# An AdaLN attention and mixture kernel: where the first batch forms its modulations, and when GpSimd builds its one-hot tables

## Chip, cores and metric

The kernel runs on one NeuronCore of a Trainium2 chip. The metric is device time in microseconds of the whole launch; lower is better. PE is TensorE, PEld its weight loads, DVE is VectorE, ACT is ScalarE, POOL is GpSimd, SP is SyncE, which here only issues DMAs.

## What is computed

The input x has 8 batches of 512 tokens with 128 channels, in fp32. Two blocks follow each other. The first is attention (8 heads of 16 channels, a top-102 emphasis of the scores, a mean over queries, a small convolution and a softmax) and a mixture of 8 experts; the second is a Mamba layer and a second mixture of 8 experts with a capacity. Both are wrapped by adaptive layer norms, whose shifts, scales and gates come from a small matrix product, once for all batches:

```python
def _layernorm(x, axis=-1, eps=1e-05):
    m = jnp.mean(x, axis=axis, keepdims=True)
    v = jnp.var(x, axis=axis, keepdims=True)
    return (x - m) / jnp.sqrt(v + eps)
...
    mod = (_silu(L0_c) @ L0_wmod).reshape(L0_c.shape[0], 6, 1, -1)
    sa, ca, ga, sb, cb, gb = (mod[:, 0], mod[:, 1], mod[:, 2], mod[:, 3], mod[:, 4], mod[:, 5])
    ga = (2 * (ga >= 0) - 1) * jnp.maximum(jnp.abs(ga), 0.25)
    gb = (2 * (gb >= 0) - 1) * jnp.maximum(jnp.abs(gb), 0.25)
    h = _layernorm(x, axis=-1) * (1 + ca) + sa
    x = x + ga * _L0_attn_ref(h, ...)
    h = _layernorm(x, axis=-1) * (1 + cb) + sb
    x = x + gb * _L0_ffn_ref(h, ...)
    mod = (_silu(L1_c) @ L1_wmod).reshape(L1_c.shape[0], 6, 1, -1)
    ...
    h = _layernorm(x, axis=-1) * (1 + ca) + sa
    x = x + ga * _L1_attn_ref(h, ...)
    h = _layernorm(x, axis=-1) * (1 + cb) + sb
    x = x + gb * _L1_ffn_ref(h, ...)
    return x
```

## The kernel before

The work of a batch is two chains. **The attention chain** prepares a batch (layer norm, the K and Q projections, a bounce of Q and K through DRAM and back into the tile qk), fills 32 score tiles of 128x512 (lines 698 on PE and 732 on ACT), and searches in five rounds for each row's threshold (line 765 on DVE, line 747 on ACT, with a few small DVE instructions such as line 772 between the rounds). The last small instruction of the search, line 781, writes g_bad. PE then runs one tiny matmul on g_bad, line 816, DVE reads its result (lines 868 to 882), and the choice phase begins: for each of the 32 tiles PE forms the scores again and masks them (lines 698 and 828), DVE takes the eight best and marks them (lines 900, 907 and 891), POOL turns the marks into weights (line 934) and PE gathers with them (line 844). A softmax phase follows, and line 1118 on DVE adds the result to x: with it a batch's attention is over.

**The rest chain** does everything else for a batch. Experts of the first mixture are pairs of fp32 matmuls, line 1307 (up) and line 1297 (down), 32 of each per batch, with a spread of the gate (line 1149) for each expert and a product on POOL between (line 1367). The Mamba part runs 32 scans (line 1566) and products (lines 1578 and 1606) with identity matmuls that sum them on PE (line 1523). Line 1138 adds the result to x, then come a layer norm, a router with many small DVE instructions (lines 1672 to 1711), and the experts of the second mixture (lines 1749, 1751, 1763 and 1828). Line 1844 adds their result and line 1864 sends the batch out.

Each engine executes its queue in order. The order in which the two chains are written into each queue is decided when the kernel is built, by `weave`: it steps through generators that yield either a signal they need or a number, an assumed duration, and keeps an assumed clock for each engine. It takes the generator that could start first; among those within 0.05 of each other it takes the one whose chain is behind. A chain's progress is the sum of the yielded numbers over its total (532.0 for the rest chain, 467.5 for the attention chain), less its lead (0.0 and 1.25). So an additional yielded number moves both the engine's assumed clock and the balance between the chains, for the whole program.

Ahead of the woven part each engine runs a setup. SP issues all loads. ACT takes the silu of the conditioning vector and the exponential of A_log. PE forms the modulation products (two groups, signal `modp`) and one product with the bias. DVE clears tables, then `dve_setup` forms the modulations from PE's two groups: 9 small instructions each, at lines 372 to 381, then lines 384 and 385. The last is the fifth rise of the signal `ready`. `started` makes every engine wait for `built`, `cleared`, `ready` and `loaded`. POOL's first work after it is `pool_one_hots` (lines 337 to 342), which builds the tables onehot and stacker; its generator then yields 20.0. The first batch's layer norm is `dve_norm` on DVE (statistics at lines 448 and 452, variance at 455), a power of -0.5 on POOL (`pool_norm`, line 467) and the normalisation on DVE at line 460.

## Time and profile before

| what | us |
|---|---|
| median of 3 runs | 3219.97 |
| lowest and highest of them | 3219.43 and 3223.93 |
| time of the profiled execution | 3232.89 |
| span of the profiled execution | 3231.7 |

The first two lines are times of ordinary executions. The profile shows another execution, of which the span is what lies between its first and its last instruction; 1.19 us of its time lie outside. The rows below come from that execution, so they are compared with its own time.

### The profile page before, as it was taken

Reading aid. Unit: us, or ns where it says so; the run is one execution under the profiler, and the core shown is the slowest. Engines: PE = TensorE matmul, PEld = TensorE weight load, DVE = VectorE, ACT = ScalarE, POOL = GpSimd, SP = SyncE. Lnnn points to the kernel's source line nnn. Section 1 sums busy time; section 2 is a strip of 40 time slices with the busy share of each in tenths; the row PEclk is TensorE's granted clock in tenths of the full one; section 3 lists DMA queues with packets and bytes.
Section 4 is the critical chain, followed back from the end, with each engine's and each line's share of the span. In section 5 each row is a group of like instructions: output and inputs, shape, how many; then the busy total and the mean of one; then the engine's idle time right before and its main releaser. Section 6 shows DMA issues by size and latency. Waiting matters only on the chain.

```text
span 3231.7 us, 34184 instructions
## 1 busy us (share of the span) xinstructions
PE 2248.2 (70%) x8658; PEld 1163.9 (36%) x8767; DVE 2569.1 (79%) x6529; ACT 1554.1 (48%) x3348; POOL 1224.5 (38%) x1118
## 2 busy tenths in 40 slices
PE   4068396877868687777768777777867778668644
PEld 2015132544234432444235522445325532345213
DVE  5974887889888898879888897979889897954482
ACT  3406633675256733676145843567236752534322
POOL 1020053623544154523544154532535144533461
PEclk8579597888978888878978788788979879779757
DMA  4011012232132312322133211323121421313222
GB/s 96 0 25 31 0 40 78 75 76 75 44 91 69 96 49 61 88 69 86 47 84 76 84 54 54 93 58 93 56 75 63 102 58 47 91 31 113 73 69 91
DMA packets 137464, 215.15 MB, mean 67 GB/s; under 512 B 17872, under 2 KB 57440, under 8 KB 134112
## 3 DMA queue, kind: packets, MB, share of 16 engines
q1 hardware_dynamic: 133088, 203.88, 23.0%
q0 software_dynamic: 4096, 8.40, 0.9%
q14 instruction: 209, 1.71, 0.2%
q8 instruction: 71, 1.16, 0.2%
HBM read 190.06 MB, written 22.15 MB: 66 GB/s over the span
## 4 chain that ended last, share of the span: by engine, by line
DVE 38%; PE 23%; issue 21%; POOL 6%; ACT 5%; DMA 2%; another core or an unknown queue 2%; DVEq 2%; SPq 1%; POOLq 0%; ACTq 0%
DVE wmask L765 13%; PE ps_att L1018 3%; DVE best L900 3%; PE ps_rest L1297 3%; PE ps_rest L1307 3%; DVE hg L1578 2%; DVE hfc L1566 2%; PE ps_att L1029 2%; POOL gat L1606 2%; DVEq L902 2%; PE ps_rest L1523 1%; PE ps_rest L1393 1%; DMA cols<-slots 1%; ACT wmask L747 1%
## 5 line engine op out<-in xcount | busy, mean ns | idle before, releaser
L765 DVE TENSOR_SCALAR_CACHE_REDUCE wmask<-z,tc 128x512 bf16<-128x512 f16 x640 | 438.8, 740 | 25.0 <-ACT z L732 22.8
L1367 POOL TENSOR_TENSOR gat<-sil,cbs 128x512 f32<-128x512 f32 x256 | 324.8, 1270 | 181.8 <-PE ps_rest L1297 114.2
L1332 ACT ACTIVATE sil<-ps_rest,w_b1T 128x512 f32<-128x512 f32 x256 | 175.7, 687 | 443.5 <-PE ps_rest L1307 424.0
L1018 PE MATMUL ps_att<-z,Vp 128*32 128x128 f32 x2048 | 290.8, 291 | 42.6 <-DVE z L1090 27.6
L934 POOL TENSOR_SCALAR wmask<-wmask 128x512 bf16<-128x512 bf16 x256 | 162.4, 634 | 381.3 <-DVE wmask L891 375.2
L1619 POOL TENSOR_TENSOR rest_c<-rest_c,hg 128x512 f32<-128x512 f32 x128 | 162.5, 1269 | 362.2 <-DVE hg L1578 362.2
L1307 PE MATMUL ps_rest<-rest_hT,WF 128*128 128x512 f32 x512 | 286.3, 646 | 7.4 <-ACT sil L1332 7.3
L1297 PE MATMUL ps_rest<-gat,WP 128*128 128x512 f32 x512 | 273.2, 617 | 6.5 <-POOL gat L1367 5.6
L1018 PEld LDWEIGHTS ps_att<-z,Vp 128*32 128x32 f32 x2048 | 213.9, 116 | 141.4 <-issue 120.6
L1523 PE MATMUL ps_rest<-hg,ident 128*128 128x512 f32 x256 | 184.1, 809 | 115.0 <-DVE hg L1578 114.8
L1068 DVE CUSTOM_DVE_ANT_0 z<-ps_att,wmask 128x512 f32<-128x512 f32 x256 | 174.9, 683 | 105.5 <-PE ps_att L1006 80.1
L1546 ACT ACTIVATE ps_rest<-cols,Aneg 128x512 f32<-128x512 f32 x256 | 175.5, 688 | 171.7 <-DVE hfc L1566 151.8
L698 PE MATMUL ps_att<-qk 128*128 128x512 bf16 x476 | 211.6, 460 | 47.0 <-DMA qk<-bounce 24.9
L1578 DVE TENSOR_TENSOR hg<-hfc,ccs 128x512 f32<-128x512 f32 x256 | 224.7, 880 | 2.6 <-POOL rest_c L1619 2.6
L467 POOL TENSOR_TENSOR rest_rstd<-rest_vpe,halfs 128x4 f32<-128x4 f32 x40 | 40.7, 1019 | 480.8 <-DVE rest_vpe L455 480.8
L900 DVE MAX8 best<-ps_att 128x8 f32<-128x512 f32 x256 | 177.3, 692 | 56.2 <-PE ps_att L828 46.8
L891 DVE SCALAR_TENSOR_TENSOR wmask<-ps_att,g_v,wmask 128x512 bf16<-128x512 f32 x256 | 192.1, 750 | 24.3 <-DVE pick L907 17.2
L1606 POOL TENSOR_TENSOR gat<-cols,cbs 128x512 f32<-128x512 f32 x128 | 179.0, 1399 | 71.9 <-DVE cols L1484 68.3
L1029 PE MATMUL ps_att<-ident,z 128*128 128x128 f32 x1024 | 178.4, 301 | 38.6 <-ACT z L1056 37.8
L1047 ACT ACTIVATE z<-z,nmx 128x512 f32<-128x512 f32 x256 | 184.9, 722 | 8.4
L1749 PE MATMUL ps_rest<-cols,WF 128*128 128x153 f32 x512 | 133.9, 346 | 71.4 <-DVE gat L1828 31.6
L1606 POOL TENSOR_TENSOR rest_c<-cols,cbs 128x512 f32<-128x512 f32 x128 | 174.8, 1366 | 0.0
(347 smaller groups left out, 5025.7 us busy)
## 6 DMA issues: line engine op xcount, KB each, us to landing
cbs<-spreads SPq DMA_DIRECT2D x128, 256.0 KB, 3.7
ccs<-spreads SPq DMA_DIRECT2D x128, 256.0 KB, 3.4
WF<-in_w SPq DMA_DIRECT2D x64, 256.0 KB, 2.6
WP<-in_w SPq DMA_DIRECT2D x64, 256.0 KB, 2.7
WF<-in_wfc SPq DMA_DIRECT2D x64, 256.0 KB, 2.6
WG<-in_wgate SPq DMA_DIRECT2D x64, 256.0 KB, 2.9
WP<-in_wproj SPq DMA_DIRECT2D x64, 256.0 KB, 3.3
qk<-bounce SPq DMA_DIRECT2D x32, 384.0 KB, 5.7
```

The lines of the kernel that those rows point to most:

```text
L698: return pe.matmul(bank[:], qs[:, h, j * P:(j + 1) * P], ks[:, h, :], start=True, stop=stop)
L765: od.up(dve.tensor_scalar(wmask[:, i, :], z_at[i], tc[:, 0, i:i + 1], None, ALU.is_ge, ALU.add, accum_out=tc[:, 1, i:i + 1]))
L891: masked.up(dve.scalar_tensor_tensor(wmask[:, i - 1, :], xbank[(i - 1) % 3][:], g_["v"][:, i - 1:i], wmask[:, i - 1, :], ALU.is_ge, ALU.add))
L900: od.up(dve.max(best[u][:, 0:8], xbank[i % 3][:]))
L1018: mm = pe.matmul(obank[o:o + 32, a * P:(a + 1) * P], Vp[:, kc, h, :], pT[u][:, kc, :], start=kc == 0, stop=kc == NT - 1)
L1029: mm = pe.transpose(in_tiles(tbank)[:, kc, :], prob[n % 2][:, kc * P:(kc + 1) * P], ident[:])
L1297: down0.up(pe.matmul(bk[3][:], W2[e % 2][:, c, :], gat[(n - 3) % 2], start=False, stop=False))
L1307: up0.up(pe.matmul(bk[n % 2][:], W1[e % 2][:, c * P:(c + 1) * P], rest.hT[:], start=True, stop=True))
L1367: weighed0.up(pool.tensor_tensor(gat[m % 2], sil[m % 2], cbs[e % 2][:], ALU.mult))
L1523: summedY.up(pe.matmul(bk[2][:], ident[:], hc[0], start=False, stop=False))
L1578: seen.up(dve.tensor_tensor(hc[k], hs[k], ccs[s % 3][:], ALU.mult))
L1606: inputs.up(pool.tensor_tensor(dBx[2 * k + s % 2], dtx[:, k, :], cbs[s % 4][:], ALU.mult))
```

## The change

The statistics of the first batch's layer norm are written ahead of the modulations on DVE, and the modulations come between the variance and the wait for POOL's power. POOL builds its one-hot tables in its setup, ahead of `started`. DVE, POOL and SP no longer wait for `ready`. Two yielded numbers change as well: the 20.0 behind the one-hot tables goes, and a 5.0 behind the modulations comes.

```diff
@@ dve_setup
         ready.up(dve.tensor_scalar(wts["bq"][:], wts["bq"][:], SCALE, None, ALU.mult))
+
+    def dve_modulations():
+
         for l in range(2):
             dve.wait_ge(*modp.at(0, l))
@@ started
         eng.wait_ge(*cleared.all(0))
-        eng.wait_ge(*ready.all(0))
+        if eng in (pe, act):
+            eng.wait_ge(*ready.all(0))
         eng.wait_ge(*loaded.all(0))
@@ dve_norm
-    def dve_norm(w, b, k, src):
+    def dve_norm(w, b, k, src, meanwhile=None):
@@
         w.var.up(dve.tensor_scalar(w.vpe[:], w.mv[:, :, 1], LN_EPS, None, ALU.add))
         yield 0.21
+        if meanwhile:
+            meanwhile()
+            yield 5.0
         yield w.rooted.at(b, k)
@@ dve_rows
-        yield from dve_norm(att, b, 0, xr[b % 3])
+        yield from dve_norm(att, b, 0, xr[b % 3], None if b else dve_modulations)
@@ pool_rest
     def pool_rest():
-        pool_one_hots()
-        yield 20.0
         for b in every:
@@
-    sp_setup(); pool_setup(); act_setup(); pe_setup(); dve_setup()
+    sp_setup(); pool_setup(); pool_one_hots(); act_setup(); pe_setup(); dve_setup()
```

The built program has the same instructions on every engine in another order. Line numbers of the changed kernel are higher by 3 from line 372 on, by 4 at lines 448 to 455 and by 7 from line 460 on. Three places show how the order changed.

The first is DVE's queue at the end of its setup. Before, the last modulations stand ahead of the statistics of the first batch's norm:

```order
L380 TENSOR_TENSOR modT<-stA,sgn 128x8
L381 TENSOR_TENSOR modT<-stA,sgn 128x8
L384 TENSOR_TENSOR bo<-ps_att,w_bo 128x1
L385 TENSOR_SCALAR gbo<-modT,bo 128x8
L448 BN_STATS att_stats<-xr 128x6 x4
L452 BN_AGGR att_mv<-att_stats 128x2 x4
L455 TENSOR_SCALAR att_vpe<-att_mv 128x4
L460 TENSOR_SCALAR att_nrm<-xr,att_mv,att_rstd 128x128 x4
```

Now, with 14 rows of modulations left out at the mark:

```order
L369 TENSOR_SCALAR w_bq<-w_bq 128x1
L452 BN_STATS att_stats<-xr 128x6 x4
L456 BN_AGGR att_mv<-att_stats 128x2 x4
L459 TENSOR_SCALAR att_vpe<-att_mv 128x4
L375 COPY modT<-ps_att 128x48
...
L384 TENSOR_TENSOR modT<-stA,sgn 128x8
L387 TENSOR_TENSOR bo<-ps_att,w_bo 128x1
L388 TENSOR_SCALAR gbo<-modT,bo 128x8
L467 TENSOR_SCALAR att_nrm<-xr,att_mv,att_rstd 128x128 x4
```

The three rows of the statistics moved ahead of all the modulations; what follows the normalisation is the same.

The second place is PE's queue around the matmul on g_bad, where the search of batch 4 (the fifth batch, counted from 0) ends. WP and WF are the expert weights, ps_att3 takes the result. Before:

```order
L1307 MATMUL ps_rest1<-rest_hT,WF_1 128x512
L1149 MATMUL ps_rest2<-cpart,onehot 128x512
L1297 MATMUL ps_rest3<-gat,WP_0 128x512
L1307 MATMUL ps_rest0<-rest_hT,WF_1 128x512
L1297 MATMUL ps_rest3<-gat,WP_1 128x512
L1307 MATMUL ps_rest1<-rest_hT,WF_1 128x512
L816 MATMUL ps_att3<-g_bad,ones_col 1x32
L1297 MATMUL ps_rest3<-gat,WP_1 128x512
L1307 MATMUL ps_rest0<-rest_hT,WF_0 128x512
L698 MATMUL ps_att0<-qk 128x512
```

Now:

```order
L1304 MATMUL ps_rest3<-gat,WP_0 128x512
L1314 MATMUL ps_rest1<-rest_hT,WF_0 128x512
L1304 MATMUL ps_rest3<-gat,WP_0 128x512
L1314 MATMUL ps_rest0<-rest_hT,WF_1 128x512
L1304 MATMUL ps_rest3<-gat,WP_0 128x512
L823 MATMUL ps_att3<-g_bad,ones_col 1x32
L1314 MATMUL ps_rest1<-rest_hT,WF_1 128x512
L1156 MATMUL ps_rest2<-cpart,onehot 128x512
L1304 MATMUL ps_rest3<-gat,WP_0 128x512
L705 MATMUL ps_att0<-qk 128x512
```

The matmul on g_bad moved back in PE's queue, past more expert matmuls. Of the batch's 32 up and 32 down matmuls 16 and 13 stood ahead of it; now it is 21 and 19, and one more spread. In batches 2 to 7 together 61 more expert matmuls and 8 more spreads stand ahead of it, in batch 1 it is 13 and 1.

The third place is DVE's queue around line 1118 (now 1125), the end of the last batch's attention. Before:

```order
L1588 SCALAR_TENSOR_TENSOR rest_c<-cols,w_m_D,rest_c 128x512
L1590 TENSOR_TENSOR hg<-rest_c,cols 128x512
L1118 TENSOR_TENSOR xr<-xr,ps_att 128x512
L1138 TENSOR_TENSOR xr<-xr,ps_rest 128x512
L448 BN_STATS rest_stats<-xr 128x6 x4
L452 BN_AGGR rest_mv<-rest_stats 128x2 x4
```

Now:

```order
L1168 TENSOR_REDUCE sv_m<-sm_t 128x4
L1169 TENSOR_TENSOR oh<-sm_t,sv_m 128x32
L1125 TENSOR_TENSOR xr<-xr,ps_att 128x512
L1687 TENSOR_TENSOR sm_oh<-oh 128x32
L1689 TENSOR_TENSOR sv_s<-sv_v 128x4
```

Behind the last line 1118 DVE had 337 instructions left, all of the rest chain; it now has 311. The 26 between them, from line 1138 to the second group of router instructions (line 1162), moved ahead of it.

## Rows read from the trace of the kernel before

**Rows 1.** The page's busy times of the whole span, with shares and instructions
```profile
PE 2248.2 (70%) x8658; PEld 1163.9 (36%) x8767; DVE 2569.1 (79%) x6529; ACT 1554.1 (48%) x3348; POOL 1224.5 (38%) x1118
```

**Rows 2.** Windows: one batch of the overlapped stretch, and the end
```profile
core 0: us, PE busy (x) PEld busy (x) DVE busy (x) ACT busy (x) POOL busy (x), PEclk, DMA share, GB/s
1408.00:1779.00 371.00, 278.27 (x1076) 144.78 (x1089) 317.43 (x797) 192.74 (x418) 150.89 (x136) 0.83 0.26 71
2873.00:3231.00 358.00, 200.66 (x708) 113.03 (x709) 165.32 (x337) 111.33 (x205) 145.51 (x119) 0.73 0.27 81
```

**Rows 3.** Timeline of the start: start, duration, engine, line, [idle before <-releaser]
```profile
8.35 0.47 SPq L295 DMA_DIRECT2D xr<-in_x  x1
...
15.43 0.21 DVE L372 COPY modT<-ps_att 128x48 f32<-128x48 f32 x1 [1.07 <-PE ps_att L355]
...
18.07 0.21 DVE L372 COPY modT<-ps_att 128x48 f32<-128x48 f32 x1 [0.94 <-PE ps_att L355]
...
19.91 0.23 DVE L385 TENSOR_SCALAR gbo<-modT,bo 128x8 f32<-128x8 f32 x1
...
20.32 0.87 DVE L448 BATCH_NORM_STATS2 att_stats<-xr 128x6 f32<-128x128 f32 x4 [0.19 <-DVE gbo L385]
20.35 0.95 POOL L337 MEMSET onehot<- 96x1024 bf16 x1 [14.78 <-DVE gbo L385]
...
21.65 0.17 DVE L455 TENSOR_SCALAR att_vpe<-att_mv 128x4 f32<-128x4 f32 x1
...
26.53 1.05 POOL L467 TENSOR_TENSOR att_rstd<-att_vpe,halfs 128x4 f32<-128x4 f32 x1
27.62 1.11 DVE L460 TENSOR_SCALAR att_nrm<-xr,att_mv,att_rstd 128x128 f32<-128x128 f32 x4 [5.80 <-POOL att_rstd L467]
```

**Rows 4.** Source view of line 295, which loads the first batch's x
```profile
DMA to landing us min/median/max: 4.8/4.8/4.8
```

**Rows 5.** Windows: the stretch ahead of the bounce transfers
```profile
30.00:35.00 5.00, 4.79 (x10) 2.73 (x11) 1.82 (x5) 1.53 (x3) 0.00 (x0) 1.00 0.00 0
```

**Rows 6.** Waits of PE from 672 to 2873 us: total, times, longest
```profile
PE ps_rest L1523 <- DVE hg L1578: 54.6, 24, 8.9
...
PE ps_att L816 <- DVE g_bad L781: 42.3, 6, 8.0
```

**Rows 7.** Waits of DVE in the same stretch
```profile
DVE best L900 <- PE ps_att L828: 34.6, 40, 2.3
```

**Rows 8.** Timeline of PE in the batch from 1408 us
```profile
1511.12 0.38 PE L1149 MATMUL ps_rest<-cpart,onehot 96*128 96x512 bf16 x1
...
1513.09 1.02 PE L1307 MATMUL ps_rest<-rest_hT,WF 128*128 128x512 f32 x2
...
1514.80 1.02 PE L1307 MATMUL ps_rest<-rest_hT,WF 128*128 128x512 f32 x2
...
1542.29 0.26 PE L816 MATMUL ps_att<-g_bad,ones_col 128*1 128x32 f32 x2 [6.92 <-DVE g_bad L781]
...
1544.35 1.91 PE L1307 MATMUL ps_rest<-rest_hT,WF 128*128 128x512 f32 x2
```

**Rows 9.** Windows: batch 1's choice; then six microseconds of batch 4's
```profile
440.00:500.00 60.00, 59.56 (x156) 21.33 (x157) 42.80 (x95) 17.46 (x27) 39.76 (x44) 0.98 0.19 54
1542.00:1548.00 6.00, 5.49 (x10) 2.17 (x12) 4.23 (x14) 0.69 (x1) 1.40 (x1) 0.50 0.07 23
```

**Rows 10.** Timeline of DVE: two issues of line 772 in batch 4
```profile
1470.58 0.16 DVE L772 TENSOR_SCALAR tc<-tc 128x14 f32<-128x14 f32 x1
...
1513.62 1.09 DVE L772 TENSOR_SCALAR tc<-tc 128x14 f32<-128x14 f32 x1
```

**Rows 11.** Timeline of POOL beside the second of them
```profile
1510.81 3.88 POOL L1367 TENSOR_TENSOR gat<-sil,cbs 128x512 f32<-128x512 f32 x3 [5.70 <-ACT sil L1332]
```

**Rows 12.** Timeline of DVE where the last batch's attention ends
```profile
2872.06 0.69 DVE L1118 TENSOR_TENSOR xr<-xr,ps_att 128x512 f32<-128x512 f32 x1 [2.24 <-PE ps_att L1105]
...
2883.38 0.19 DVE L1162 TENSOR_TENSOR oh<-sm_t,sv_m 128x32 bf16<-128x32 f32 x1
```

## The prediction

> **What bounds the kernel now.** I read the busy shares first. DVE is busy 79% of the span, PE 70%, ACT and POOL less than half [rows 1]. The windows say where that holds: a batch in the overlapped stretch takes 371 us and DVE is busy 317 of them, while the last 358 us, in which the rest chain runs alone, keep DVE busy for only 165 [rows 2]. So the kernel has three kinds of time: a start that is a pure chain of waits, seven batches in which DVE is nearly full, and an end that is a chain again. A microsecond taken from the start or the end counts whole. In the middle only DVE's waits can be won or lost.
>
> The start is next. In its timeline the normalisation of the first batch (line 460) waits 5.80 us for POOL's power, the power stands behind the one-hot tables, and these wait 14.78 us for line 385, the last rise of `ready` [rows 3]. That is the chain which the diff speaks of. The waits of the middle are third, since the order listings show that the change reaches there: PE waits 42.3 us in six pieces at line 816 for the end of the search, and DVE waits 34.6 us in 40 pieces for the masked scores of line 828 [rows 6, 7].
>
> **The start.** DVE is through with line 369 at 15.43 - 1.07 = 14.36 us. The first batch's x was issued at 8.35 and took 4.8 to land, so it is there at 13.15 [rows 3, 4]. The statistics can start at 14.36. They took from 20.32 to 21.65 + 0.17 = 21.82, that is 1.50 us, and will end at 15.86. The first group of modulations lasts from 15.43 to 18.07 - 0.94 = 17.13, 1.70 us; it now runs from 15.86 to 17.56. The second group waits for PE's products, which let it go at 18.07 [rows 3], and PE is not touched. So the slack of 0.51 us swallows the displaced group, and line 385 ends at 19.91 + 0.23 = 20.14 as before. POOL's power takes 1.05 us [rows 3] and runs at about 16 to 17 beside the modulations. The normalisation starts at about 20.2 in place of 27.62: 7.4 us earlier.
>
> The one-hot tables cost nothing where they now stand. They took POOL from 20.35 to 26.53, 6.2 us, and POOL was idle for 14.78 us before them, since 5.6 us [rows 3]; they end at about 12, ahead of the power at 15.9. Without that cover they would cost their 6.2 us, which is what they cost before. The waits that DVE, POOL and SP lose are of no further price. PE and ACT keep theirs, and both are released at 20.14 ahead of their first work.
>
> One thing can take some of it back. Line 772 takes 0.16 us, but 1.09 when it was issued at 1513.62 beside a POOL product, and it ended at 1514.71, when POOL's group ended at 1510.81 + 3.88 = 1514.69 [rows 10, 11]. A small DVE instruction can thus be held by a POOL instruction. If the power holds the first group for its whole 1.05 us, that group ends at 18.61, 0.54 behind the slack, and the gain is 6.9. I take 7.0, with 6.9 and 7.4 as bounds. The Trainium skill ("SBUF — State Buffer", section "Who interferes with whom") says that DVE and GpSimd share a pair of ports, that an instruction with two SBUF inputs contends with a GpSimd instruction that reads SBUF, and that the loser blocks fully. By that rule the sum would be at 6.9 if such an instruction of the group meets the power, and at 7.4 if only the others do.
>
> What follows moves with it. Next in the chain are the bounce transfers. The DMA engines moved nothing from 30 to 35 us [rows 5], ahead of the first bounce, so bounces that start 7 us earlier meet free queues.
>
> **The middle.** The two yielded numbers change the planner's balance: 20/532 less progress for the rest chain and 5/467.5 more for attention, 0.048 batches together in favour of the rest chain. In the listings this is seen at line 816. In batches 2 to 7, 61 more expert matmuls and 8 more spreads stand ahead of it. A pair of expert matmuls starts every 1514.80 - 1513.09 = 1.71 us, so one is worth 0.86, and a spread is at most 0.38 [rows 8]: 61 x 0.86 + 8 x 0.38 = 55.5 us of work. PE was idle there for 42.3 us [rows 6] and fills that. The other 13 us delay the matmul on g_bad, by about 2 us a batch, and DVE has little else in its queue there: this is a cost, +13.
>
> Against it stand two gains. Behind the idle stretch PE's granted clock was 0.50 from 1542 to 1548, the lower of its two levels (1.2 GHz) [rows 9], and the pair that follows line 816 was done at 1544.35 + 1.91 = 1546.26 [rows 8], 3.8 us after it started in place of 1.7. With no idle stretch there is no such fall. DVE's own small instructions between line 816 and the first choice run beside, so I count 1 of the 2.1 us, -6 in six batches. And PE has 42 us less to do in the six choice phases. DVE's waits for line 828, 34.6 us [rows 7], are the ones that expert matmuls ahead of an attention tile cause. Nothing in the trace says how many of them go. I take a third, -12, for POOL and DVE hand tiles to each other in the same phase. Together +13 - 6 - 12 = -5. The bounds are +13, if nothing is given back, and 13 - 12 - 35 = -34, if all is.
>
> In batch 1 there is no idle stretch to fill, and 13 matmuls and a spread (11.6 us) delay line 816. But from 440 to 500 us PE is busy 59.56 of 60 [rows 9]. There PE is the bound, and doing the same work in another order costs nothing, so 0.
>
> **The end.** 26 DVE instructions of the rest chain move ahead of the last line 1118. Before, they took from 2872.06 + 0.69 = 2872.75 to 2883.38 + 0.19 = 2883.57, 10.8 us [rows 12]. In the end stretch DVE is busy 165.32 / 358.00 = 0.46 of the time [rows 2], so 5.0 of the 10.8 are work, which must now be done earlier, and 5.8 are waits, which other work now covers: -6, between 0 and -10.8.
>
> **The sum** is -7 - 5 - 6 = -18 us. The profiled execution took 3232.89, which becomes 3214.9. The median of the runs is 12.9 lower, 3219.97, which becomes 3202.
>
> **The rivals.**
>
> *Only the start is gained.* The middle and the end even out: 3219.97 - 7 = 3213. For it speaks that DVE is busy 317 of 371 us, and reordering does not shorten its work; against it, that the end is a chain and loses 26 instructions. This lies just beyond 0.2%, which is 6.4 us and about what a measurement of this kernel can tell from no change.
>
> *The wait at line 816 moves to DVE and stays (slower).* The place is the end of every search: DVE writes g_bad, and PE is still at expert matmuls. Before, PE was always there first. If the delay is D a batch and nothing returns, six batches cost 6 D, and with the +7 to be repaid and another 6.4 to show, it decides from D = 2.2 us. My row-based D is 2.1 and would be near 4 if batch 1's 11.6 us came in too: -7 + 13 + 11 = +17, 3237; with batch 1 left out, 3226. I give 3232 as its middle. Against it: the clock and the lighter choice phase.
>
> *PE's idle time is won whole.* All 42.3 us appear in the end time, with start and end: 3219.97 - 7 - 34 - 6 = 3173, or about half of it, 3190. Against it: DVE, not PE, is the fuller engine.
>
> *The scans stand badly.* PE already waits 54.6 us in 24 pieces for the Mamba products at line 1523 [rows 6], with attention matmuls queued behind. The listings put these rows up to 50 attention rows earlier. Two further waits of the same 2.3 us a batch would be 28 us: 3219.97 - 18 + 28 = 3230.
>
> *It does not do what it says.* Something in the start, such as the bounce transfers, takes the 7 us back, and the rest evens out: 3220. The free queues speak against it.
>
> **How the numbers follow.** Chances: the forecast 0.42, with a range of its own from 3193 to 3210; only the start 0.19; the middle won in half or whole 0.13; the wait at line 816 0.13; the scans 0.07; nothing 0.06. Faster by over 0.2% are the forecast, the won middle and two thirds of the second case: 0.68. Within 0.2% are the rest of that case and the last: 0.12. Slower are the two cases that say so: 0.20. The range must reach to the half-won middle on one side and take in part of the two slower cases on the other: 3185 to 3229.
>
> **What would show it.** In the profile of the changed kernel POOL's one-hot rows stand before 12 us, the power at about 16, the normalisation at about 20.2 and the first search 7 us earlier. PE's wait at the matmul on g_bad is near zero in batches 2 to 7, its clock does not fall behind it, and DVE shows a new wait of 2 to 3 us there. The overlapped batch still takes about 370 us, and the end behind line 1125 is some 11 us shorter. If the interval of the batches grows by 2 us or more, the forecast is wrong, and it is wrong the other way if the interval falls by 3 or more.

## The result, and the profile after

| kernel | median us (lowest to highest) | runs | ratio to before, 95% interval |
|---|---|---|---|
| before | 3221.95 (3207.39 to 3225.11) | 6 | 1 |
| changed | 3272.47 (3267.82 to 3275.07) | 6 | 1.0152, 1.0133 to 1.0171 |

The change makes the kernel 1.5% slower, where 0.6% faster was forecast. The profiled execution of the changed kernel took 3275.07 us and its span is 3273.8, which is 42.1 more than before. The medians lie 50.5 us apart: the profiled execution of before was 10.9 us above its median here, that of the changed kernel 2.6. The page's busy times:

```profile
PE 2247.6 (69%) x8650; PEld 1160.9 (35%) x8767; DVE 2599.0 (79%) x6529; ACT 1551.6 (47%) x3348; POOL 1230.2 (38%) x1118
```

DVE runs the same 6529 instructions as in [rows 1] and is busy 30 us longer with them. The timeline of the start, as in [rows 3]:

```profile
14.47 0.87 DVE L452 BATCH_NORM_STATS2 att_stats<-xr 128x6 f32<-128x128 f32 x4
...
16.13 1.06 POOL L474 TENSOR_TENSOR att_rstd<-att_vpe,halfs 128x4 f32<-128x4 f32 x1 [4.52 <-DVE att_vpe L459]
...
16.84 0.21 DVE L381 TENSOR_TENSOR stA<-modT,sgn 128x48 f32<-128x48 f32 x1
...
18.19 0.21 DVE L375 COPY modT<-ps_att 128x48 f32<-128x48 f32 x1 [0.63 <-PE ps_att L355]
...
20.18 1.11 DVE L467 TENSOR_SCALAR att_nrm<-xr,att_mv,att_rstd 128x128 f32<-128x128 f32 x4
```

The start does what was forecast. The power runs from 16.13 to 17.19 beside the modulations, none of them is stretched, the second group still starts when PE lets it go, and the normalisation is at 20.18, 7.4 us earlier. The first batch's attention ends (the end of line 1125, line 1118 before) 8.0 us earlier, at 308.3 instead of 316.3 us. The last stretch, from the end of the last line 1125 to the end of the span, went from 359.0 to 346.4 us, 12.6 less; about 11 was forecast. What lies between grew by 62.7 us: the seven intervals between the ends of the attention were 356, 365, 371, 371, 371, 367 and 355 us and are 357, 377, 373, 384, 385, 384 and 359. -8.0 + 62.7 - 12.6 = +42.1.

The waits of PE from 672 to 2928 us (engine, line, releaser: total, times, longest), to be held against [rows 6]:

```profile
PE ps_att L851 <- POOL wmask L941: 79.3, 67, 6.5
PE ps_rest L1530 <- DVE hg L1585: 66.5, 20, 9.7
PE ps_att L823 <- DVE g_bad L788: 55.9, 6, 12.3
```

The first of them, the wait of the gather for POOL's weights in the choice, was shorter by 34.5 us in the kernel before, from 672 to 2873 us:

```profile
PE ps_att L844 <- POOL wmask L934: 44.8, 53, 4.2
```

It is no measure of the loss: in e3_with20 below, which is faster than before, it is 71.8 us.

And of DVE, against [rows 7]:

```profile
...
DVE best L907 <- PE ps_att L835: 30.3, 26, 2.8
DVE hg L1835 <- ACT hfc L1794: 27.3, 27, 4.4
DVE gat L1835 <- ACT hfc L1794: 26.4, 19, 5.1
...
DVE sm_lg L1679 <- PE ps_rest L1173: 13.9, 6, 3.1
```

PE's wait for g_bad, which was to vanish, has grown from 42.3 to 55.9 us, in six pieces still. DVE's wait for the masked scores fell by 4 us only. At line 1835, the gate product of the second mixture's experts, DVE waits 53.7 us for ScalarE's line 1794, where it was 23.0 before. For the router's product, at line 1679, it waits 13.9 us, where it was 2.8.

The first experiment below is the changed code with the old numbers in the planner, so its order is that of before. Windows over the same batch, phase by phase (search, choice, softmax), first in it:

```profile
1394.00:1525.00 131.00, 93.87 (x357) 54.63 (x357) 119.22 (x395) 92.47 (x214) 37.54 (x34) 0.80 0.25 77
1525.00:1619.00 94.00, 80.25 (x202) 27.57 (x206) 76.93 (x186) 21.46 (x32) 43.30 (x51) 0.91 0.13 39
1619.00:1763.00 144.00, 102.80 (x518) 60.49 (x527) 122.18 (x218) 78.78 (x173) 69.54 (x51) 0.86 0.34 89
```

and in the changed kernel:

```profile
1416.00:1556.00 140.00, 101.53 (x362) 61.00 (x364) 121.08 (x377) 95.14 (x218) 41.21 (x36) 0.82 0.25 74
1556.00:1655.00 99.00, 72.83 (x183) 23.98 (x188) 84.46 (x192) 24.77 (x34) 43.05 (x51) 0.86 0.17 50
1655.00:1799.00 144.00, 103.40 (x531) 60.95 (x538) 116.88 (x231) 72.31 (x166) 68.81 (x52) 0.87 0.31 78
```

The search is 9 us longer and DVE has fewer instructions in it (377 for 395), so there it waits more. In the choice DVE is busy 7.5 us more for 6 more instructions: the timelines show which work. In the choices of batches 2 to 7 together stand 20 of the 192 scans and 10 of the products behind them (line 1585), where before and e1_oldnum have none. In the searches stand 124 of the 192 GpSimd products of the first mixture (line 1374), where those two have 94.

The same three phases over batches 2 to 7, summed from each kernel's timeline, say where each of the kernels below gains or loses. The search lasts from the end of the addition to x of the batch before to the end of line 788, the choice from there to the end of the last line 898, the softmax from there to the end of line 1125. All three lines are DVE's, numbered as in the changed kernel. Two more columns give batch 1 as a whole and the last stretch, in us:

| kernel | search | choice | softmax | batch 1 | last stretch |
|---|---|---|---|---|---|
| before | 806 | 555 | 840 | 356 | 359 |
| e1_oldnum | 800 | 553 | 840 | 348 | 359 |
| changed | 845 | 584 | 833 | 357 | 346 |
| e2_newnum | 843 | 585 | 833 | 358 | 348 |
| e6_hold | 832 | 601 | 829 | 358 | 346 |
| e7_short_new | 795 | 581 | 833 | 356 | 345 |
| e8_short_old | 781 | 544 | 834 | 345 | 356 |
| e13_hold_scans | 842 | 570 | 839 | 360 | 353 |
| e14_hold_route | 846 | 581 | 810 | 356 | 350 |
| e15_early_route | 805 | 562 | 893 | 363 | 345 |
| e18_route_short | 794 | 576 | 804 | 353 | 348 |

Each row is one execution. The pairs of one order, before with e1_oldnum and changed with e2_newnum, differ by up to 6 us in a phase and 7 in batch 1. Against e1_oldnum the changed kernel loses 45 us in the searches and 31 in the choices, and none in the softmax phases.

### The profile page after: what moved, and what is told of

It is laid out like the page before. It is cut to its first block and busy times, and to the rows that moved or that the text cites. A ratio compares the mean times of both kernels' runs of the same rounds, so it can differ in the third digit from the quotient of the medians.

```text
span 3273.8 us, 34165 instructions
## 1 busy us (share of the span) xinstructions
PE 2247.6 (69%) x8650; PEld 1160.9 (35%) x8767; DVE 2599.0 (79%) x6529; ACT 1551.6 (47%) x3348; POOL 1230.2 (38%) x1118
## 5 line engine op out<-in xcount | busy, mean ns | idle before, releaser
L1314 PE MATMUL ps_rest<-rest_hT,WF 128*128 128x512 f32 x512 | 293.2, 660 | 42.3 <-ACT sil L1339 39.0
L1530 PE MATMUL ps_rest<-hg,ident 128*128 128x512 f32 x256 | 191.7, 840 | 130.3 <-DVE hg L1585 130.3
L705 PE MATMUL ps_att<-qk 128*128 128x512 bf16 x468 | 204.9, 456 | 35.3 <-DMA qk<-bounce 18.6
L851 PE MATMUL ps_att<-wmask,Qpad 128*64 128x512 bf16 x256 | 115.1, 461 | 142.3 <-POOL wmask L941 110.1
```

Of the source, the lines that this page charges most:

```text
L705: return pe.matmul(bank[:], qs[:, h, j * P:(j + 1) * P], ks[:, h, :], start=True, stop=stop)
L1314: up0.up(pe.matmul(bk[n % 2][:], W1[e % 2][:, c * P:(c + 1) * P], rest.hT[:], start=True, stop=True))
L1530: summedY.up(pe.matmul(bk[2][:], ident[:], hc[0], start=False, stop=False))
```

## The experiments

The kernels ran in groups, each beside the kernel before, which took 3219.16 us (experiment 1), 3225.42 (2 and 3), 3220.02 (4), 3222.43 (5) and 3218.0 (6) as medians. Differences between groups are therefore taken from ratios: 0.01 is 32 us.

**1. Code or numbers.** Four kernels part the moved code from the two yielded numbers. `e1_oldnum` is the changed code with both numbers as before, `e2_newnum` the code of before with both new numbers, `e3_with20` the changed kernel with the 20.0 alone put back, and `e5_lead` the changed kernel with the balance shifted back by the lead.

```diff
 e1_oldnum, dve_norm
-            yield 5.0
 e1_oldnum and e3_with20, pool_rest
+        yield 20.0
 e5_lead, weave
-           (467.5, 1.25, (("pe", pe_choices()), ...
+           (467.5, 1.298, (("pe", pe_choices()), ...
```

> The changed kernel with the yielded numbers of before: POOL's generator yields 20.0 again and the 5.0 behind the modulations is gone. The queues of PE, ACT, POOL and SP are then those of before, and DVE's differs in its first 27 rows alone. Theory A (the move of the code is good, the new order of the woven part costs): the start gains 7.5 to 8 us and nothing else changes, 3221.95 - 7.5 = 3214, between 3209 and 3218. Rival B (the moved code itself does harm later, by the dropped waits on ready or by POOL's tables in the setup): it stays at 3240 or above, up to the 3272 of the changed kernel.

> The kernel before with only the yielded numbers of the change: the 20.0 goes, and a 5.0 comes behind the variance of the first batch. No instruction of the start moves; the woven part has the order of the changed kernel. Theory A (the new order costs): 3272.5 + 7.5 = 3280, between 3273 and 3286. Rival B (the moved code costs): 3222, as before. If both had a part, it lies between, and the two kernels show whether the parts add up.

> The changed kernel with the 20.0 on POOL given back and the 5.0 kept: the balance is then off by 5/467.5 = 0.011 batches in place of 0.048. If the cost is in proportion to the shift of the balance: 3214 + 58 x 0.22 = 3227. If any disturbance of the order costs about the same, since the order of before is a lucky one: 3250 or more. If small shifts cost nothing: 3214.

> The changed kernel with a lead of 1.298 in place of 1.25, which gives back the 0.048 batches by which the balance between the chains moved. PE's queue then differs from before in 456 of 5950 rows, in place of 3547. Theory A1 (the balance of the chains is what costs): 3214, within 6 us. Rival A2 (what costs is the assumed clock of POOL, which starts 20 lower): the time stays above 3245.

| kernel | median us | ratio, 95% interval |
|---|---|---|
| e1_oldnum | 3213.42 | 0.9984, 0.9968 to 1.0 |
| e2_newnum | 3283.0 | 1.0199, 1.0182 to 1.0216 |
| e3_with20 | 3199.07 | 0.9929, 0.9908 to 0.9949 |
| e5_lead | 3199.85 | 0.9945, 0.9925 to 0.9964 |

The loss is in the order that the two numbers make: 1.0152 - 0.9984 = 0.0168, 54 us. The moved code itself gains some 5 us by e1_oldnum, and 0.0047, 15 us, by e2_newnum, which has the changed kernel's order without its code (each with an interval of 5 to 8 us to either side). A balance shifted by 0.048 of a batch costs 54 us. One shifted by 5/467.5 = 0.011, e3, costs nothing and is even faster. So the loss does not grow evenly with the shift.

**2. Hold the second mixture's experts.** In the changed order they are woven into the stretch in which ScalarE refills the 32 score tiles and then takes the first signs: in six batches only 32, 22, 22, 17, 13 and 13 of the 32 refills stand ahead of their first line 1794, where all 32 did before. `e6_hold` holds them behind the first round of the search. The added yields of this and the later holds only tell the planner when a generator may go on; no engine gets a wait.

```diff
     def pe_experts1(b):
+        if b + 2 < B:
+            yield aim.at(b + 2, 1)
```

> The changed kernel with one more yield, at the start of pe_experts1, that lets the writer of the order place the experts of the second mixture of batch b only when batch b+2's balance has passed one round; no engine gets a wait from it. In the order, ScalarE's whole refill of batch b+2 (32 instructions) again stands ahead of the first line-1794 instruction, as in the kernel before, where the changed kernel has 32, 22, 22, 17, 13, 13. Theory R (the cost is that the second mixture's experts are woven into ScalarE's refill and sign burst, so that VectorE waits at its head for hfc): VectorE's waits of L1835 for ScalarE fall from 38 us to below 16 us, and the time comes back to 3215 to 3235. Rival S (the cost is the order of the experts of the first mixture, or more small VectorE instructions beside GpSimd's products, and the waits for hfc are only where it shows): the waits move to other lines and the time stays at 3255 or above.

It took 3276.67 us, ratio 1.0167 (1.0148 to 1.0186). DVE's waits from 672 to 2926 us in it:

```profile
...
DVE tc L779 <- ACT wmask L754: 34.8, 7, 8.0
```

The waits at line 1835 are gone from the list and the time is not. DVE now waits 34.8 us for ScalarE's signs (line 779), where it was 10.4. In the table the searches are 13 us shorter and the choices 17 longer. The theory that this one meeting is the cause fell.

**3. GpSimd's products, and a third of the shift.** `e7_short_new` and `e8_short_old` shorten GpSimd's product of the first mixture to 64 of 512 columns (line 1374 of the changed code), in the changed order and in that of e1; the product of the other 448 columns is left out, and they hold a constant. `e9_lead1265` gives back a third of the shift.

```diff
-                weighed0.up(pool.tensor_tensor(gat[m % 2], sil[m % 2], cbs[e % 2][:], ALU.mult))
+                weighed0.up(pool.tensor_tensor(gat[m % 2][:, 0:64], sil[m % 2][:, 0:64], cbs[e % 2][:, 0:64], ALU.mult))
```

> The changed kernel with GpSimd's product of line 1374 on 64 of its 512 columns (the rest of the tile holds what one memset left there, so the output is not the reference's); the order of instructions is the changed kernel's. To be read against e8_short_old. Theory C (contention: small VectorE instructions are stretched beside GpSimd's products, 30 us more of them in the changed kernel): VectorE's busy time falls more here than in e8, and the gap of the two is 25 to 35 us where the gap of the full kernels was 59 us. Theory R (ScalarE's refill and the experts collide in the order): GpSimd's product is no part of it, and the gap stays at 50 us or more.

> The same shortening of GpSimd's product of line 1374 to 64 of 512 columns (output not the reference's) in e1_oldnum, the changed code with the yields' numbers of before, which took 3213. Theory C: 3170 to 3200, with e7 25 to 35 us above it. Theory R: e7 50 us or more above it.

> The changed kernel with a lead of 1.265, so that an order arises in which only the last three batches' second-mixture experts stand inside ScalarE's refill (32, 32, 32, 22, 22, 17 refill instructions ahead of the first line-1794 instruction). Theory R: a time between the two groups, 3225 to 3245, with the batches' lengths back to those of before in the first three and long in the last three. Rival S: no relation to those positions; near 3200 or near 3270.

| kernel | median us | ratio, 95% interval |
|---|---|---|
| e7_short_new | 3211.78 | 0.9955, 0.994 to 0.997 |
| e8_short_old | 3172.68 | 0.9845, 0.9826 to 0.9863 |
| e9_lead1265 | 3231.17 | 1.0016, 1.0003 to 1.0029 |

With short products the gap between the orders is 0.0110, 35 us, instead of 54. That lies between the two expectations: some 19 us of the loss hang on the length of these products. The source view of one small DVE instruction of the search shows how (count: lowest/median/highest ns), first in the changed kernel, then in e7_short_new:

```profile
L791 DVE COPY_PREDICATED lo_tc<-gi_over,tc x32: 232/234/1321, 77.0 to 2681.3; 128x64 f32<-128x64 int32 x32
```

```profile
L792 DVE COPY_PREDICATED lo_tc<-gi_over,tc x32: 232/233/386, 76.9 to 2625.4; 128x64 f32<-128x64 int32 x32
```

and GpSimd's product in the two, in the same way:

```profile
L1374 POOL TENSOR_TENSOR gat<-sil,cbs x256: 1257/1268/1430, 394.0 to 3058.5; 128x512 f32<-128x512 f32 x128
```

```profile
L1375 POOL TENSOR_TENSOR gat<-sil,cbs x256: 308/319/449, 393.1 to 3002.8; 128x64 f32<-128x64 f32 x128
```

An instruction of 0.23 us takes up to 1.3 beside a product of 1.27, and at most 0.39 beside one of 0.32. In the changed kernel six of the 32 take over 1.1 us, and each of the six ends 0.09 us behind the end of a product; in e1_oldnum it is one of 32. That follows from the 30 additional products in the searches. DVE's busy time says the same for all instructions: from full to short products it falls from 2599.0 to 2519.5 us in the new order and from 2573.2 to 2514.0 in the old, 79.5 and 59.2, so the new order has 20 us more of such holding. And the table has it where the loss is: the searches of the two orders differ by 45 us with full products and by 14 with short ones, the choices by 31 and 37. A shorter product also reaches PE sooner; no run separates the two ways.

**4. Three holds.** Compared with before, three places stood otherwise: the second mixture's experts (above), the first mixture's experts (only 46, 36, 36, 31, 34, 32 and 22 of the 50 signs of the next search ahead of their first silu, before 50, 50, 50, 49, 47, 44 and 36), and the scans (ahead of the last 1 to 5 masks of the choice). `e10_hold_first` holds the first mixture's experts, `e11_hold_both` adds the hold of e6_hold, `e12_hold_three` that of the scans, `e13_hold_scans` has the last alone.

```diff
     def pe_experts0(b):
+        if b + 1 < B:
+            yield aim.at(b + 1, 4)
     def dve_states(b):
+        if b + 1 < B:
+            yield masked.at(b + 1, TILES - 1)
```

> The changed kernel with a yield at the start of pe_experts0 that lets the writer of the order place the experts of the first mixture of batch b only when batch b+1's balance has come to its last round; no engine gets a wait from it. All 50 sign instructions of the search then stand ahead of ScalarE's first silu, as in most batches of the kernel before (changed: 46, 36, 36, 31, 34, 32, 22). The experts of the second mixture and the scans stay where the changed kernel has them. Theory F (the experts of the first mixture, placed beside ScalarE's sign bursts and beside small VectorE rounds, are what costs): 3210 to 3235. Theory M (two or three meetings cost together, each about a third): 3250 to 3265. Theory U (the whole offset of the two chains matters and no single place): 3265 to 3285.

> Holds of e10_hold_first and of e6_hold together. Theory F: 3210 to 3235, no better than e10. Theory M: 3230 to 3245. Theory U: 3265 to 3285.

> Both holds and a third, at the start of dve_states, that keeps the scans of batch b behind the last mask of batch b+1's choice in the order, as all seven batches of the kernel before have it (the changed kernel places them 1 to 5 tiles before the choice is through). Theory M: 3205 to 3230, since the three meetings are undone. Theory F: as e10. Theory U: 3260 or more, since the chain of the second layer is only pressed together and not moved back against the attention's.

> The third hold alone: the scans of batch b behind the last mask of batch b+1's choice, all else as in the changed kernel. If the scans between the last choices of tiles are the cost (the choices were 5 to 8 us longer in the changed kernel): 3225 to 3245. If not: 3265 to 3285.

| kernel | median us | ratio, 95% interval |
|---|---|---|
| e10_hold_first | 3324.24 | 1.0322, 1.0296 to 1.0348 |
| e11_hold_both | 3287.51 | 1.0221, 1.0194 to 1.0249 |
| e12_hold_three | 3283.9 | 1.0206, 1.0183 to 1.0229 |
| e13_hold_scans | 3273.37 | 1.0164, 1.0142 to 1.0187 |

None is faster than the changed kernel, and holding the first mixture's experts costs some 55 us more. The hold of e6_hold, which alone gave nothing, gives 0.0101, 32 us, when it is added to that of e10. The hold of the scans moves time without saving it: the choices are 14 us shorter, the softmax phases 6 longer and the last stretch 7. A hold seems to leave a hole: what filled the engines there in the old order has already been done, and does not come back. That is a reading, and no run tests it.

**5. The routing.** What filled DVE's queue at these places in the old order is the next candidate. These are rows of DVE's timeline at the start of the search of batch 4, in e1_oldnum:

```profile
1392.50 0.69 DVE L1124 TENSOR_TENSOR xr<-xr,ps_att 128x512 f32<-128x512 f32 x1 [0.27 <-PE ps_att L1111]
1393.62 0.74 DVE L771 TENSOR_SCALAR_CACHE_REDUCE wmask<-z,tc 128x512 bf16<-128x512 f16 x1 [0.44 <-ACT z L738]
...
1395.86 0.19 DVE L1678 TENSOR_TENSOR sm_lg<-ps_rest,w_router_b 128x32 f32<-128x32 f32 x1 [0.81 <-PE ps_rest L1172]
...
1402.57 0.16 DVE L1717 TENSOR_TENSOR sv_p<-sv_p,sv_r 128x4 f32<-128x4 f32 x1
```

and in the changed kernel:

```profile
1405.01 0.19 DVE L1679 TENSOR_TENSOR sm_lg<-ps_rest,w_router_b 128x32 f32<-128x32 f32 x1 [2.77 <-PE ps_rest L1173]
...
1407.88 0.42 DVE L1091 COPY och<-ps_att 128x256 f32<-128x256 f32 x1
...
1410.79 0.17 DVE L1718 TENSOR_TENSOR sv_p<-sv_p,sv_r 128x4 f32<-128x4 f32 x1
...
1414.47 0.69 DVE L1125 TENSOR_TENSOR xr<-xr,ps_att 128x512 f32<-128x512 f32 x1 [3.12 <-issue]
1415.60 0.75 DVE L772 TENSOR_SCALAR_CACHE_REDUCE wmask<-z,tc 128x512 bf16<-128x512 f16 x1 [0.44 <-ACT z L739]
```

Before, the small instructions that route the second mixture's tokens stand behind the attention's last addition, in ScalarE's refill. Now they stand ahead of it. DVE waits 2.77 us for the router's product, and the attention's last steps (line 1091 and what follows to line 1125) queue behind. In the refill there is then nothing left for DVE but the comparisons of the search (line 772, which some of the expectations call scans too) and the experts that wait for ScalarE. In the orders of e1, e3 and e5 the routing stands behind the addition in all batches, in those of the changed kernel, of e2_newnum, e7_short_new and of experiments 2 and 4 it stands ahead in the first six at least, and in e9_lead1265 (3231 us) it stands ahead in five of seven. Two kernels moved the routing: `e14_hold_route` back in the changed kernel, `e15_early_route` forward in e1_oldnum. In both the second mixture's experts moved with it, to behind all 32 refills in e14 and to behind 25 of them in e15. `e16_lead131` moves the whole chain further back.

```diff
 e14_hold_route, dve_mixture1, behind the normalisation
+        if b + 1 < B:
+            yield attended.at(b + 1)
 e15_early_route, dve_project, ahead of line 1124
+        if b:
+            yield shares.at(b - 1)
 e16_lead131, weave
-           (467.5, 1.25, (("pe", pe_choices()), ...
+           (467.5, 1.31, (("pe", pe_choices()), ...
```

> The changed kernel with a yield in dve_mixture1, between the normalisation and the routing, that lets the writer of the order place the 22 small VectorE instructions of the routing of batch b only behind the attention's last addition of batch b+1 (line 1125), where all fast orders have them; no engine gets a wait. In the order the second mixture's experts then fall behind ScalarE's whole refill by themselves (32 in all six batches), while the scans (30 and 27 of 32 tiles) and the first mixture's experts (36 of 50 signs) stay where they are or nearly. Theory W (VectorE has this work, which needs little of ScalarE, for the 20 us of ScalarE's refill, and with it gone ahead it delays the attention's end and leaves the refill to experts that wait for ScalarE at each step): 3200 to 3235. Theory U (the offset of the chains as a whole): 3265 or more, as with the other holds.

> The changed code with the yields' numbers of before (e1_oldnum, 3213) and one yield at the start of dve_project that lets the writer place the attention's last addition of batch b only behind the routing of batch b-1, where the changed kernel has it; no engine gets a wait. The second mixture's experts then begin with 25 of ScalarE's 32 refills ahead, the scans stay behind the choice (32), and the first mixture's experts behind 42 to 50 signs in six of seven batches. Theory W: 3240 to 3275. Theory U: 3205 to 3230.

> The changed kernel with a lead of 1.31 (1.298 took 3200): the rest's chain still further back against the attention's, the routing 2 to 10 scans into the search. Theory W: a plateau on this side, 3190 to 3210. Theory U with a cost that grows with the distance from one best offset: 3215 to 3240.

| kernel | median us | ratio, 95% interval |
|---|---|---|
| e14_hold_route | 3254.41 | 1.0099, 1.0072 to 1.0126 |
| e15_early_route | 3274.13 | 1.0158, 1.0131 to 1.0185 |
| e16_lead131 | 3194.36 | 0.9921, 0.9896 to 0.9945 |

Moving the routing forward costs 0.0174, 56 us, and moving it back in the changed kernel returns 0.0053, 17 us. DVE's waits in e15_early_route, from 672 to 2928 us:

```profile
DVE hg L1836 <- ACT hfc L1795: 35.6, 39, 2.8
...
DVE sm_lg L1680 <- PE ps_rest L1174: 29.5, 6, 10.3
...
DVE gat L1836 <- ACT hfc L1795: 14.4, 10, 2.6
```

and in e1_oldnum, from 672 to 2853:

```profile
DVE hg L1834 <- ACT hfc L1793: 20.9, 13, 4.5
```

The 56 us look like the 54 of the changed kernel, and the table says that they are others. e15 loses 53 us in the softmax phases, where the changed kernel loses none, and 5 in the searches, where the changed kernel loses 45. Its hold forces the attention's end behind a routing that is not ready: DVE waits 29.5 us for the router's product, where the changed kernel waits 13.9. The likeness of the two sums is chance.

e14 says what the place costs in the changed kernel. Its softmax phases are 23 us shorter, and its searches as long as before the hold, 846 for 845 us, though DVE is busy 22 us more in them. So the routing costs nothing in ScalarE's refill, and 23 us where it stands ahead of the attention's end. Against e1_oldnum the choices of e14 are 28 us longer and its softmax phases 30 shorter: the scans that moved from the one to the other nearly even out. An empty refill is not what makes the search longer: e14 filled it again without shortening the search, and e15 emptied it at a cost of 5 us. The waits for hfc, which rise from 22.1 us in e1 (1.2 of them at gat) to 50.0 in e15, near the 53.7 of the changed kernel, do not make it longer either, since in e15 the search hardly is.

**6. Do the parts add?** `e17_hold_route_first` is e14 with the hold of e10, `e18_route_short` is e14 with the short product of experiment 3, `e19_before_lead` is the kernel before with a lead of 1.262, which gives it nearly the order of e16.

> e14_hold_route with the yield of e10_hold_first as well: routing behind the attention's end, and the experts of the first mixture behind all 50 signs. If what is left in e14 (3254 against 3213) is the place of the first mixture's experts: 3215 to 3235. If holding them only makes the chain of the second layer late, as it did alone (3324 against 3272): 3265 to 3310.

> e14_hold_route with GpSimd's product of line 1374 on 64 of its 512 columns, as in e7_short_new (3212) and e8_short_old (3173); output not the reference's. If the loss has two parts that add, the routing's place (about 19 us) and the stretching of VectorE's instructions beside GpSimd's products (about 20 us, the shrinking of the gap from 59 to 39), this takes 3185 to 3200. If the two are one effect seen twice: about 3212, no better than e7. If there is a third part of about 20 us that neither covers, it also stays some 20 us above e8: 3190 to 3197.

> The kernel before with the lead of 1.262, which gives it nearly the order of e16_lead131 (the routing at +10, +7, +6, +6, +2, +2 scans in both). If the moved code is worth its 6 to 8 us also in this order, this takes 3198 to 3208, above e16's 3194 by 6 to 10. If the order is all of the gain over before: 3190 to 3197.

| kernel | median us | ratio, 95% interval |
|---|---|---|
| e17_hold_route_first | 3301.45 | 1.024, 1.0207 to 1.0273 |
| e18_route_short | 3185.69 | 0.9894, 0.9867 to 0.9921 |
| e19_before_lead | 3199.74 | 0.9934, 0.9913 to 0.9954 |

With short products, moving the routing back gives 0.9955 - 0.9894 = 0.0061, 20 us, as much as with full ones. So the two parts add. e18 is still 0.0049, 16 us, above e8_short_old. Of the 54 us, 17 go with the routing's place (and that of the second mixture's experts, which moved with it), 19 with the length of GpSimd's products, and the other 18 (16 by e18) with neither. The interval of each of these differences is 10 to 13 us to either side. In the table e18 is 13 us longer than e8 in the searches and 8 in batch 1; its choices are 32 longer and its softmax phases 30 shorter, the move of the scans again. Holding the first mixture's experts as well costs again, as in experiment 4. And e19 says that most of e16's gain over before is the order: at nearly the same order the moved code is worth 0.9934 - 0.9921 = 0.0013, 4 us, less than the intervals tell apart.

## Why the prediction was wrong

**The start, -7.0.** Right in every step. 7.4 is the upper of its two bounds. The modulation with two SBUF inputs at 16.84 took 0.21 us while the power ran, so what the prediction took from the Trainium skill ("SBUF — State Buffer", section "Who interferes with whom") for such an instruction did not come out here. The bounce transfers took nothing back. In the run time the moved code shows 5 us (e1, 0.0016, with an interval from 0 to 10), 15 us (the changed kernel against e2, 7 to 23) and 4 us (e19 against e16).

**The end, -6.** The stretch behind line 1125 is shorter by 12.6 us, as the step said (11). That the work has to be done earlier was counted too, at 5.0 us. What was missed is where.

**The middle, -5 (bounds -34 to +13).** This is the step that failed: it came out at +62.7, or +56 when the 6.6 us that the end gave beyond its 6 are set against it. Three statements of it fell:

- "PE was idle there for 42.3 us [rows 6] and fills that." The idle time is 55.9 us. The step left the search where it was and put more PE work ahead of line 823. But the search became longer, by 4 to 8 us in each of batches 2 to 7 and 39 in all, and PE, with its additional work done, waited for it again. Idle time in front of a wait belongs to the chain that ends last there, which is DVE's.
- "With no idle stretch there is no such fall." The idle stretch stayed and the fall with it: in batch 4 the up matmul right behind line 823 (two records) took 2.08 us, where it is 1.91 in [rows 8], and 1.02 for those at 1513 us there. The granted clock was 0.55 from 1556 to 1560 us.
- "I take a third, -12" of DVE's waits for line 828. They fell by 4.3 us, and the choices became 29 us longer, of which the step had nothing: 20 scans had moved into them. That is nearly given back in the softmax phases, which lost the scans.

The step failed because it was read at one line of PE's queue, while DVE was named as the full engine. It left out two things. With the 61 expert matmuls, 30 of GpSimd's products moved from the choices into the searches, beside the small instructions on which the search depends. The prediction had such a held instruction in [rows 10] and [rows 11], and priced it at the start alone; in the search it was put at nothing. With short products 31 of the 45 us by which the searches of the two orders differ are gone. The other is the order of DVE's queue. The third place shown with the change was the last batch's routing moving ahead of line 1118, and it was priced as a gain of the end. The same move stands in the other batches, where it is a loss: it delays the attention's end by work that cost nothing in ScalarE's refill, 23 us by e14. The prediction looked at it once, where nothing follows the attention.

**The rivals.** "The wait at line 816 moves to DVE" gave slower, 3232, by another mechanism; DVE got no new wait at the choice. "PE's idle time is won whole" fell with the idle time, which grew; its sum also takes 34 us, the bound of the middle, where its words say 42.3. "The scans stand badly" is not it: e13_hold_scans moved them back and left the time as it was, and PE's wait at line 1530 rose from 54.6 to 66.5 us only. "Only the start is gained", 3213, is what e1_oldnum did, that is, the change without its two numbers. What the prediction said would show it wrong did so: the batches' interval grew by 13 us at batch 4 where 2 was the mark.

**What stays open.** Some 16 us of the 54 have a place and no cause: with the routing back and the products short, the searches are still 13 us longer than in e8 and batch 1 is 8 us longer, the latter hardly more than two kernels of one order differ. A candidate is the first mixture's experts, which begin inside ScalarE's last sign bursts; the holds can't weigh them, because a hold costs by itself. Nor does a run move the routing without the second mixture's experts, or the products without the expert matmuls around them. And e3_with20 and e5_lead are faster than e1_oldnum by 0.004 to 0.006 at orders that differ little from it. No run separates why.

## What to carry over

When a change moves a written order, look for each moved piece in every batch and on the engine that is the bound, and ask of it what it was hiding, what it now stands in front of and what comes to stand beside it. A piece that shortens the tail may be the filler of a stretch in the loop, and one run that loses the same sum is not yet the same loss: compare where the time goes, phase by phase. A number yielded to a planner is a change of its own: here 5 us of moved code were paid with 54 us of order, and putting the balance back (e5_lead, or a lead of 1.31) made the same code 0.6 to 0.8% faster than before. And a hold that puts a piece back at its old place does not put back what used to stand ahead of it.

## What the runs showed of the hardware

A small DVE instruction can be held for the length of a GpSimd one. With GpSimd's 256 products at 1.27 us, DVE is busy 2599.0 us; with the products at 0.32 us the same 6529 instructions take 2519.5 us (e7_short_new). That is 80 us of DVE time from an engine that is busy 38% of the span, and the kernel was 0.0197, 63 us, faster. In the old order it is 59.2 us of DVE time and 0.0139, 45 us. The held instruction of experiment 3 copies under a mask with tiles in SBUF only, and its longest time follows that of the product, 1321 and 386 ns against medians of 1268 and 319. All six long ones of the changed kernel end 0.09 us behind a product's end. The Trainium skill ("SBUF — State Buffer", section "Who interferes with whom") says that DVE and GpSimd share a pair of ports and that whoever issues first has it for the whole instruction while the other blocks fully. On the block to the end of the instruction the trace agrees. What the Trainium skill says there does not explain why the power at 16.13 us held none of the modulations; no run here tells what differs.
